# Attention with a mixture-of-experts layer: VectorE's small work moved between cosines and sines, weight pieces in other heads, scores between the projections

## What is computed

```python
q = rope(einsum('bsd,dnh->bsnh', norm(x), wq)) / sqrt(128)
k = rope(einsum('bsd,dnh->bsnh', norm(x), wk))
v = einsum('bsd,dnh->bsnh', norm(x), wv)
probs = softmax(where(causal, einsum('bqnh,bknh->bnqk', q, k), -1e30))
x = x + einsum('bqnh,nhd->bqd', einsum('bnqk,bknh->bqnh', probs, v), wo)

h = norm(x)                                  # rows, 2048 x 256
scores = softmax(h @ gate_w.T)               # 8 experts
topk_w, topk_idx = top_k(scores, 2)
y = sum over the two experts of weight * (silu(h @ w1[e]) * (h @ w3[e])) @ w2[e]
x = x + y + (silu(h @ sw1) * (h @ sw3)) @ sw2
```

## Time and profile before

| | |
|---|---|
| median of 3 runs | 726.54 us (725.61 to 727.05) |
| the profiled execution | 725.12 us, of which the span of instructions is 723.3 us |
| PE busy | 715.9 us, 99% of the span |
| DVE busy | 621.3 us, 86% |
| ACT busy | 524.6 us, 73% |
| POOL busy | 507.5 us, 70% |
| granted PE clock | full speed in all slices |
| chain that ended last | PE 91%, of which the line L662 69% |

### The profile page before, as it was taken

How to read it: one execution, slowest core, us unless ns; L and a number is a source line. 1 busy time by engine, 2 the same in 40 slices (tenths; PEclk the granted TensorE clock), 3 DMA queues, 4 the chain that set the end, 5 groups by cost and what they waited for, 6 DMA issues and landing times.

```text
span 723.3 us, 16479 instructions
## 1 busy us (share of the span) xinstructions
PE 715.9 (99%) x5482; PEld 689.0 (95%) x5482; DVE 621.3 (86%) x1774; ACT 524.6 (73%) x1664; POOL 507.5 (70%) x539
## 2 busy tenths in 40 slices
PE   8999999999999999999999999999999999999997
PEld 8999999999999999999999999999999999999997
DVE  6888899989998999899989998999898976866657
ACT  5887777777777777777777777777777765666564
POOL 4997467787777777877778787777866623544545
PEclk9999999999999999999999999999999999999999
DMA  6664204321332143214321421130454384344383
GB/s 214 162 185 162 79 31 141 114 81 37 135 112 84 45 136 119 78 46 144 117 72 47 148 99 62 38 108 32 126 203 164 156 268 129 117 124 133 103 300 102
DMA packets 51212, 85.92 MB, mean 119 GB/s; under 512 B 8632, under 2 KB 43416, under 8 KB 49528
## 3 DMA queue, kind: packets, MB, share of 16 engines
q1 hardware_dynamic: 47080, 73.44, 30.6%
q0 software_dynamic: 4048, 11.42, 4.4%
...
## 4 chain that ended last, share of the span: by engine, by line
PE 91%; POOL 2%; DVE 2%; issue 1%; ACT 1%; DMA 1%; SPq 1%; ACTq 0%; POOLq 0%; DVEq 0%
PE bank L662 69%; PE bank L712 5%; PE bank L721 4%; PE bank L702 4%; PE bank L952 1%; PE bank L933 1%; POOL w_lo L1876 1%; DMA stage<-in_L_attn_wk 1%; POOL work L489 1%; PE bank L849 1%; PE bank L908 1%; PE bank L964 1%; PE bank L968 1%; PE bank L969 1%; PE bank L965 1%
## 5 line engine op out<-in xcount | busy, mean ns | idle before, releaser
L489 POOL TENSOR_TENSOR work<-work 128x512 f32<-128x512 f32 x126 | 163.2, 1295 | 52.0 <-DVE work L1104 51.3
L1802 POOL TENSOR_TENSOR qkt_lo<-work,qkt_hi 128x512 fp32r<-128x512 f32 x112 | 144.8, 1293 | 70.5 <-ACT qkt_hi L1560 70.3
L1104 DVE TENSOR_TENSOR work<-bank,sinn 64x512 f32<-64x512 f32 x256 | 176.1, 688 | 3.4
L662 PE MATMUL bank<-xnt_hi,w_lo 128*128 128x256 f32 x512 | 148.6, 290 | 1.0 <-DVE xnt_lo L1440 0.9
L662 PE MATMUL bank<-xnt_lo,w_hi 128*128 128x256 f32 x512 | 144.9, 283 | 0.0
L662 PE MATMUL bank<-xnt_hi,w_hi 128*128 128x256 f32 x512 | 144.8, 283 | 0.0
L1560 ACT CAST qkt_hi<-work 128x512 fp32r<-128x512 f32 x112 | 69.5, 621 | 97.2 <-POOL work L489 97.2
L1567 ACT ACTIVATE work<-work,bias 128x128 f32<-128x128 f32 (+1 forms) x256 | 112.7, 441 | 0.4 <-DVE bias L1113 0.4
L1097 DVE TENSOR_TENSOR work<-bank,cosn 128x512 f32<-128x512 f32 x128 | 87.9, 687 | 20.0 <-PE bank L662 19.8
L662 PEld LDWEIGHTS bank<-xnt_hi,w_lo 128*128 128x128 f32 x512 | 97.7, 191 | 2.8 <-DVE xnt_lo L1440 1.1
L662 PEld LDWEIGHTS bank<-xnt_hi,w_hi 128*128 128x128 f32 x512 | 98.1, 192 | 0.4
...
## 6 DMA issues: line engine op xcount, KB each, us to landing
...
```

Of the source, the lines that this page charges most:

```text
L489: eng.tensor_tensor(roped[:, a], rope_cos[:, a], rope_sin[:, a], ALU.add).then_inc(rope_add, 1)
L662: mm = pe.matmul(out, lhs[a], rhs[b], start=start and n == 0, stop=stop and n == 2, skip_group_check=more)
L1104: op = nc.vector.tensor_tensor(rope_sin[lo:lo + 64, a], p_qk[a][hi:hi + 64, :, :], sn, ALU.mult)
L1802: nc.gpsimd.tensor_tensor(qkt[a][1][:, :, :], roped[:, a], qkt[a][0][:, :, :], ALU.subtract).then_inc(qkt_lo, 1)
```

## The change

- VectorE: the two `row_norm` of the previous sequence's rows, which stood one after head 2's `att_lo` and one after head 3's, both stand in head 3 between the cosines and the sines. In the last sequence both stood after head 2's `att_lo` and now stand there too. The compare (head 6; head 5 in the last sequence) and `norm_x` of the next rows (head 9) move from behind `att_lo` to between cosines and sines of their head.
- Weight pieces: heads 0, 4, 6, 10, 12 instead of 0, 2, 4, 8, 10. GpSimd subtracts one head later, but two heads later for the piece of head 12.
- PE: the projection of h+4 is cut in two (q, then k), and the scores of h+2 stand between the halves instead of ahead of both. In head 12 the scores stay ahead. A wait for the rope products of head h+2 is added ahead of the first half.
- ScalarE: in head 11 `xnt_high` stands ahead of the exponentials.

```diff
@@ split_schedule
-            heads += [(b, h) for b in range(1, LAST) for h in (0, 2, 4, 8, 10)]
+            heads += [(b, h) for b in range(1, LAST) for h in (0, 4, 6, 10, 12)]
@@ tensor: project
-            def project(h, first=False):
+            def project(h, parts=(0, 1), first=False):
-                for m in range(2):
+                for m in parts:
...
-                mm.then_inc(qk_ps, 1)
+                if parts[-1] == 1:
+                    mm.then_inc(qk_ps, 1)
@@ tensor: sequence
+                    if b is not LAST or h + 4 < N:
+                        if b is FIRST and h in (0, 2, 4, 6, 8, 10):
+                            wait_pieces(pe, pieces_for("heads", h))
+                        if h != 12:
+                            pe.wait_ge(rope_mul, j0 + h + 3)
+                            project((h + 4) % N, (0,))
+                    if b is not LAST or h + 2 < N:
                         scores(j0 + h + 2)
                     if b is not LAST or h + 4 < N:
                         if h == 12:
                             pe.wait_ge(xnt_lo, b + 2)
-                        if b is FIRST and h in (0, 2, 4, 6, 8, 10):
-                            wait_pieces(pe, pieces_for("heads", h))
-                        project((h + 4) % N)
+                            project(0)
+                        else:
+                            project((h + 4) % N, (1,))
@@ vector: sequence
                         rope_cosines((h + 4) % N)
+                        if b is not FIRST and h == 3:
+                            rows_norm(b, b - 1)
+                        if b is not FIRST and h + soon == 6:
+                            compare(b)
+                        if b is not LAST and h == 9:
+                            norm_x(b + 1)
                         rope_sines((h + 4) % N)
...
-                        if h == 2:
-                            if b is LAST:
-                                rows_norm(b, b - 1)
-                            else:
-                                dve.wait_ge(rstd2_done, b)
-                                row_norm(b - 1, 0)
-                        if h == 3 and b is not LAST:
-                            row_norm(b - 1, 1).then_inc(xn2_done, 1)
-                        if h + soon == 6:
-                            compare(b)
...
-                        if h == 9:
-                            norm_x(b + 1)
@@ scalar: sequence
+                    if h == 11 and b is not LAST:
+                        xnt_high(b + 1)
                     if b is not LAST or h + 2 < N:
                         exps(j0 + h + 2, (h + 2) % N)
-                    if h == 11 and b is not LAST:
-                        xnt_high(b + 1)
@@ gpsimd: sequence
-                    for n in split_now(b, h - 1):
+                    for n in split_now(b, h - 1 if b is FIRST or h < 13 else h - 2):
```

## The result

Before: median 726.08 us (725.37 to 727.05, 4 runs beside the changed kernel). After: median **736.81 us** (736.40 to 737.97, 4 runs). The ratio is 1.0145, 95% interval 1.0131 to 1.0159. The span of the profiled execution went from 723.3 to 734.8 us. The forecast was 730.0 us with a range up to 733.8: the sign was right, the size was not.

The account below looks back on a forecast made before the run. PE's own work, 4.33 us per undisturbed head, was taken as the bound. Middle sequences +3.4, a wide piece +0.34, first -0.4, last +0.15 made +3.5 us, so 730.0 us; own range 728.0 to 732.2, full range 723.5 to 733.8.

Parts of the forecast that it names:

- the piece in head 14: GpSimd's low part of a weight piece there, 0.94 or 1.28 us, fits the room: s of head 15 0.4 to 0.8, cost nothing.
- norms in head 3: VectorE's two norms cost 1.5 us, L1125 of heads 3 and 4 starts in time: 0.31 saved, 0.05 lost in head 4.
- limit 1.93: Latest start of GpSimd's L489 in head 4 without delaying PE's next transposes; usually 1.5, this head has 0.43 more of transposes.
- The rule of the port: VectorE or GpSimd, whichever starts first, fully blocks the other; a norm ahead of L1802 could add 1.2 us in all.
- the list of limits: Two limits per head: VectorE's L1125 may start at +2.47, GpSimd's L489 at 1.5 at most, before PE waits.
- Compare: In head 6 it waits for L1802, L489 of head 7 becomes 1.25; with head 7's piece, head 8 is 0.2 over.
- rival 1: Faster: the chain of head 7 does not form, VectorE's norm and compare win against L1802; 722.8 us, chance 0.18.
- Heads 9 and 10: VectorE's rank waits for late L1897, L1125 starts at +2.94 in both: 0.47 lost each, against 0.12 now in head 10.
- Rival 3: Worse: the port rule, a wider piece, or head 14's split meeting the scatters of heads 15 and 0; 733.5 us, chance 0.12.
- Scores between the projections: On PE, gain 0, bounds 0 and 0.02 per head; masks 0.3 later, covered by VectorE's 0.41 idle before the cosines.
- Rounding sooner: ScalarE's 1.0 us of exponentials in head 11 leaves the next rows' path, so head 12's 0.19 wait goes; 1.1 us gained.
- First and last sequence: First: norms free of weight pieces sooner, -0.4; last: norms ahead of L1125 of head 3, 0.45 against 0.6 if moved, +0.15.

Follow-up runs that it names:

- n_rows: b_scores_round with only the rows' norms moved, both in head 3 between cosines and sines: 726.29 us, 1.0006 against the kernel before.
- a_clear_sooner: The changed kernel with each of SyncE's clears of the scatters' table issued one piece sooner: 732.94 us, 1.0100 against the kernel before.
- a_clear_spread: The changed kernel with each clear's access pattern given an outer dimension of 16, not 4: 733.87 us, 1.0092 against the kernel before.
- b_pieces: The kernel before with only the weight pieces and GpSimd's split rule of the change: 735.39 us, ratio 1.0115.
- a_oldpieces: The changed kernel with pieces and split rule of before, so scores and rounding edits stay in: 729.90 us, 1.0033 against the kernel before.
- n_next: b_scores_round with only the next rows' norm put in front of the sines of head 9: 728.27 us, 1.0034 against the kernel before.
- b_scores_round: The kernel before with only the scores between the projection halves and the next rows rounded sooner: 724.66 us, ratio 0.9970.
- b_scores: The kernel before with only the scores between the two halves of the projections: 725.63 us, ratio 0.9987.

## Why the prediction was right or wrong, step by step

Two places that the sum put at nothing made the miss: the piece in head 14 (+6.3 us in heads 0 to 2) and head 5 behind the norms (+3.5). Without them the span would have grown by 1.7 us, little more than the 1.45 that a measurement can tell from no change.

- *Heads 3 and 4, norms in head 3: right.* Both norms took 1.71 us (forecast 1.5) and ended 0.16 after L1804. L489 of head 4 came at +2.04 (forecast +1.9, limit 1.93), and head 4 itself lost nothing by it, where 0.05 was forecast. Forecast -1.6 (six times 0.26), measured -1.48, of which the shorter heads are some 0.25.

```profile
255.65 1.71 DVE L1267 TENSOR_SCALAR xn<-resid,mv,rstd 128x256 f32<-128x256 f32 x2
255.77 1.43 POOL L1804 TENSOR_TENSOR qkt_lo<-work,qkt_hi 128x512 fp32r<-128x512 f32 x1 [0.73 <-ACT qkt_hi L1562]
...
258.86 1.30 POOL L489 TENSOR_TENSOR work<-work 128x512 f32<-128x512 f32 x1 [1.66 <-DVE work L1112]
```

  The rule of the port which the forecast weighed (the Trainium skill, "SBUF — State Buffer", "Who interferes with whom") is borne out for the norm behind GpSimd's operations of 0.9 to 1.4 us, of which it ended 0.14 to 0.16 us later each time. The other way round, L1804 with a norm in front of it took 1.43 instead of 1.29: later by 0.14, where the first norm, 255.65 to about 256.06, overlaps it by 0.29. A full block would have cost 0.29.
- *What becomes of head 4's lateness: the step that failed first.* I followed it to the next transposes and stopped, since head 4 was inside its limit. It went on to head 5 through ScalarE and the masks, and met there a taker that the list of limits did not have: the logits (+3.50 us, forecast 0). n_rows shows it alone (+3.45): PE waits for the end of the masks, and the list had only the low part.
- *Compare: no loss in head 8, where 0.2 was forecast.* In sequence 3, L489 of head 7 came at +1.06 (forecast +1.25) and of head 8 at +1.50 (forecast +1.7). The chain formed, against rival 1, but 0.2 us shorter than worked out, and so head 8 ended just inside the limit of 1.5 instead of 0.2 over it: no loss, forecast 1.2 us and 0.34 for the wide piece. The compare took 0.74 in head 6 and ended at +3.88.
- *Heads 9 and 10: near in sum (3.9 for 4.9), half right in cause.* L1899 ended at +1.68 (forecast +1.65), and L1133 started at +2.96 (forecast +2.94):

```profile
281.64 0.46 POOL L1899 TENSOR_TENSOR xn<-xn 128x128 f32<-128x128 f32 x1
...
283.39 0.41 DVE L1133 TENSOR_TENSOR pt_lo<-bank,pt_hi 128x256 fp32r<-128x256 f32 x1
...
283.86 0.39 PE L662 MATMUL bank<-pt_hi,v_lo 128*128 128x256 f32 x1 [0.24 <-DVE pt_lo L1133]
```

  That is sequence 3, where head 9 is 4.83 long (forecast 4.80). Three of the six are at 4.78 or more, the others at 4.45 to 4.57, so the sum is 1.89 for 2.8. It is 0.76 with the pieces alone (b_pieces) and -0.12 with VectorE's moves alone (a_oldpieces), so most of it needs both; no run has the pieces with the compare and nothing else. Head 10 is at 5.09 to 5.12 (+1.99, forecast 2.1), but the wait there is for the values' low part, 288.04 in sequence 3, and n_next shows it with no piece and no compare moved. In a_oldpieces it is even larger (+3.29), with head 9 undisturbed. That a late head 9 gives VectorE time is my reading; no run tries it.
- *Piece in head 14, "cost nothing": wrong, +6.3.* This is the largest miss. The step counted GpSimd's own 0.94 or 1.28 us against the room of one head, and took that room from head 13 of rows 2, where L1802 ends at +3.8. In head 14 a scatter stands in front: in sequence 3 of the kernel after, L1804 ended at +4.18, and L489 of head 15 came at +1.07, not at the forecast's 0.4 to 0.8. It also left out that the scatters of 1.0 us in the heads that follow leave no room to give it back (2.9 us in heads 0 to 2, a_clear_sooner and a_clear_spread), and that moving the pieces moves what SyncE does behind them (the other 3.4). Rival 3 named the place, "a split in head 14 that meets the scatters of heads 15 and 0", and with 733.5 came nearest, at a chance of 0.12 and with too small a price: up to 0.3 on two heads of six sequences, where it was 1.06 a sequence. (At its full prices, 1.2 and 3.6, it would have said 734.8, outside the range; 733.5 counts 3.5 in all.)
- *Scores between the projections: right in kind.* Priced at 0 with bounds up to a loss of 0.02 a head; it was a gain of 0.02 a head. In undisturbed heads the masks' cover of 0.41 sufficed; in heads 2 to 4 it fell 0.1 us a sequence short (b_scores_round). My bounds had left out a gain without a reason for that.
- *Rounding sooner: right.* Forecast -1.1, measured -1.1 (head 12, b_scores_round against b_scores). Head 12 of sequence 3 in the kernel after:

```profile
295.03 0.69 DVE L1143 TENSOR_TENSOR xnt_lo<-bank,xnt_hi 128x512 fp32r<-128x512 f32 x1
295.10 0.49 PE L713 MATMUL bank<-ident,work 128*128 128x128 f32 x3
```

  The next rows' low part now starts 0.07 ahead of head 12's transposes; in rows 6 it started 0.24 behind them.
- *First and last sequence.* -0.09 for -0.4: the norm gave its 0.3 (n_next against its base: -0.33), and the scores took 0.25 there (b_scores), 0.5 of it in head 2. Last: +0.82 for +0.15, 0.29 from VectorE's norms (a_oldpieces), the rest from the same head 2.

In all, heads 0 to 2 and 5, which had no term, made 9.8 us, and everything else together 1.7, where +3.5 was said.
